# Top-k masks of an attention kernel: another form of the instruction, and all of them on GpSimd

## What is computed

```
q, k = layernorm(q), layernorm(k)              # over the 8 columns of a head
scores = q @ k.T / sqrt(8)                     # 256 x 256 for each batch and head
aw = softmax(scores)
kth = top_k(aw, 12)[..., -1:]                  # int(256 * 0.05) = 12
aws = aw * (aw >= kth)                         # keep the 12 largest of each row
o_s = (aws / (aws.sum(-1) + 1e-8)) @ v
```

## Time and profile before

| | us |
|---|---|
| median of 3 runs | 1230.13 (1228.34 to 1232.35) |
| the profiled execution, whole | 1228.88 |
| its span, first instruction to last | 1226.5 |
| busy: VectorE | 1187.3 (97%) |
| busy: ScalarE | 1086.7 (89%) |
| busy: GpSimd | 1083.7 (88%) |
| busy: TensorE | 962.0 (78%) |
| DMA, mean share of its 16 engines | 22.9% |

### The profile page before, as it was taken

How to read it: one execution, slowest core, us unless ns; L and a number is a source line. 1 busy time by engine, 2 the same in 40 slices (tenths; PEclk the granted TensorE clock), 3 DMA queues, 4 the chain that set the end, 5 groups by cost and what they waited for, 6 DMA issues and landing times.

```text
span 1226.5 us, 34671 instructions
## 1 busy us (share of the span) xinstructions
PE 962.0 (78%) x8997; PEld 653.9 (53%) x9028; DVE 1187.3 (97%) x4553; ACT 1086.7 (89%) x3626; POOL 1083.7 (88%) x1688
## 2 busy tenths in 40 slices
PE   2577878877788788788787878778887888788786
PEld 1255555555556555565555555555555555555554
DVE  6699999999999999999999999999999999999994
ACT  2498999999999999999999989999999999999984
POOL 4599999999999999999999999999999999999964
PEclk9999999999999999989999999999999999999989
DMA  2122212222221222221222221222222122222110
GB/s 62 48 74 79 83 46 65 61 80 83 83 70 43 67 70 83 83 79 41 71 60 83 83 84 45 66 58 83 83 83 65 50 66 71 83 83 79 38 52 14
DMA packets 165143, 82.78 MB, mean 67 GB/s; under 512 B 7753, under 2 KB 164943, under 8 KB 164946
## 3 DMA queue, kind: packets, MB, share of 16 engines
q1 hardware_dynamic: 164946, 80.56, 22.9%
HBM read 42.78 MB, written 37.75 MB: 66 GB/s over the span
## 4 chain that ended last, share of the span: by engine, by line
DVE 60%; issue 26%; PE 4%; DVEq 4%; POOL 3%; ACT 2%; SPq 0%; DMA 0%; POOLq 0%; ACTq 0%
DVE rest L539 26%; DVE top L532 20%; DVE next L545 8%; DVEq L75 4%; POOL below L386 2%; PE turn_ps L834 1%; DVE o_sparse L587 1%; ACT e L717 1%; DVE lin_z L560 1%; DVE den L584 1%; PE pv_ps L855 0%; PE turn_ps L835 0%; DVE stats L595 0%; PE work_ps L932 0%; DVE den L579 0%
## 5 line engine op out<-in xcount | busy, mean ns | idle before, releaser
L386 POOL TENSOR_SCALAR below<-e,next 128x256 bf16<-128x256 f32 x800 | 725.8, 925 | 0.5 <-issue 0.4
L717 ACT ACTIVATE e<-score_ps,drop 128x256 f32<-128x256 f32 x1024 | 472.9, 481 | 57.1 <-POOL drop L364 53.8
L834 PE MATMUL turn_ps<-ident,e 128*128 128x128 f32 x2048 | 401.0, 289 | 40.6 <-ACT kept L687 17.8
L539 DVE MATCH_REPLACE8 rest<-e 128x256 f32<-128x256 f32 x1024 | 409.7, 402 | 0.0
L545 DVE MAX8 next<-rest 128x8 f32<-128x256 f32 x1024 | 403.1, 406 | 0.6 <-issue 0.3
L835 PE MATMUL turn_ps<-minus_huge,below 128*128 128x128 bf16 x2048 | 380.1, 225 | 0.0
L532 DVE MAX8 top<-score_ps 128x8 f32<-128x256 f32 x1024 | 358.4, 408 | 6.8 <-PE score_ps L816 6.6
L834 PEld LDWEIGHTS turn_ps<-ident,e 128*128 128x128 f32 x2048 | 297.6, 145 | 78.9 <-issue 33.0
L687 ACT ACTIVATE kept<-turn_ps 128x1024 f32<-128x1024 f32 x256 | 267.8, 1046 | 39.3 <-PE turn_ps L835 38.9
L835 PEld LDWEIGHTS turn_ps<-minus_huge,below 128*128 128x128 bf16 x2048 | 222.3, 109 | 0.8 <-issue 0.2
L717 ACT ACTIVATION_READ_ACCUMULATOR e<-score_ps,drop 128x1 f32 x1024 | 217.4, 212 | 0.0
(11 more groups left out here) (156 smaller groups left out, 1333.2 us busy)
## 6 DMA issues: line engine op xcount, KB each, us to landing
part_slots<-part SPq DMA_DIRECT2D x128, 192.0 KB, 2.3
q_slots<-part_slots SPq DMA_DIRECT2D x64, 256.0 KB, 3.3
k_slots<-part_slots SPq DMA_DIRECT2D x64, 256.0 KB, 4.1
part_slots<-part SPq DMA_DIRECT2D x64, 128.0 KB, 1.9
x_sb<-in_L_attn_x SPq DMA_DIRECT2D x32, 128.0 KB, 4.2
x_res<-in_L_attn_x SPq DMA_DIRECT2D x32, 128.0 KB, 4.1
out_y<-out_sb SPq DMA_DIRECT2D x32, 128.0 KB, 4.4
w_ops<-in_L_ffn_W SPq DMA_DIRECT2D x1, 512.0 KB
```

Of the source, the lines that this page charges most:

```text
L386: nc.gpsimd.tensor_scalar(below[:, r, t, :], e[:, r, t, :], next8[:, r, t, TOPK - 9:TOPK - 8], None, ALU.is_lt).then_inc(s["below_pool"], 1)
L539: nc.vector.match_replace(rest[:, t, :], e8[:, (u_ - 1) % 2, t, :], e[:, (u_ - 1) % RING, t, :], REMOVED).then_inc(s["rest_ready"], 1)
L717: nc.scalar.activation(e[:, u_ % RING, t, :], score_ps[:, u_ % 2, t // 2, t % 2, :], ACT.Exp, bias=drop[:, u_ % 2, t, 0:1], accum_out=z[:, ...
L834: mm(dst, e[:, r, t, keys], ident[:], start=True, stop=False, is_transpose=True)
```

## The change

All masks go to GpSimd, and ScalarE's are removed. The form for nearly all units, called `gap`: for each tile `gap` = e x (-1) + limit (one instruction with two operations, bf16 result), a wait until the four are done, then one instruction for the unit: `below` = max(gap, 0) over 4 x 256 columns. So `below` is zero or positive, as ScalarE's form was. The first four units of the run use four other forms:

- unit 0, `least`: min(e, limit) - limit, one instruction a tile; the result is zero or negative, so `turn` multiplies with a diagonal of +2^40, the new constant `plus_huge`;
- unit 1, `compare`: (e < limit) x 1.0, one instruction a tile;
- unit 2, `clamp`: `gap` as above, then min(max(gap, 0), 2^40) over the unit;
- unit 3, `wide`: `gap` by one subtraction of two tensors over the unit, the limit repeated along the columns, then max(gap, 0).

`gap` has two buffers. TensorE waits for one count, `below_ready`, instead of two.

```diff
-POOL_TILES = (3, 2, 3, 4, 4, 4, 3, 2)
+FIRST_FORMS = ("least", "compare", "clamp", "wide", "gap", "gap", "gap", "gap")
...
+            nc.gpsimd.memset(plus_huge[:], 0.0).then_inc(s["pool_step"], 1)
+            select(plus_huge[:], ALU.not_equal, HUGE, 0, [[-1, P]], 1, 9).then_inc(s["gather_ready"], 1)
...
-                        for t in range(POOL_TILES[r]):
-                            wait_alone(pool, s["next_ready"], TILES * (g - 2) + t + 1, s["waits_passed"])
-                            nc.gpsimd.tensor_scalar(below[:, r, t, :], e[:, r, t, :],
-                                                    next8[:, r, t, TOPK - 9:TOPK - 8], None,
-                                                    ALU.is_lt).then_inc(s["below_pool"], 1)
+                        form = FIRST_FORMS[r] if g - 2 < UNITS else "gap"
+                        if form in ("least", "compare"):
+                            for t in range(TILES):
+                                limit = next8[:, r, t, TOPK - 9:TOPK - 8]
+                                pool.wait_ge(s["next_ready"], TILES * (g - 2) + t + 1)
+                                if form == "least":
+                                    nc.gpsimd.tensor_scalar(below[:, r, t, :], e[:, r, t, :], limit, limit, ALU.min,
+                                                            ALU.subtract).then_inc(s["below_ready"], 1)
+                                else:
+                                    nc.gpsimd.tensor_scalar(below[:, r, t, :], e[:, r, t, :], limit, 1.0, ALU.is_lt,
+                                                            ALU.mult).then_inc(s["below_ready"], 1)
+                        else:
+                            half = u_ % 2
+                            if form == "wide":
+                                pool.wait_ge(s["next_ready"], TILES * (g - 1))
+                                nc.gpsimd.tensor_tensor(gap[:, half], next8[:, r, :, TOPK - 9:TOPK - 8].to_broadcast(
+                                    [P, TILES, N]), e[:, r], ALU.subtract).then_inc(s["gap_step"], 1)
+                            else:
+                                for t in range(TILES):
+                                    pool.wait_ge(s["next_ready"], TILES * (g - 2) + t + 1)
+                                    nc.gpsimd.tensor_scalar(gap[:, half, t, :], e[:, r, t, :], -1.0,
+                                                            next8[:, r, t, TOPK - 9:TOPK - 8], ALU.mult,
+                                                            ALU.add).then_inc(s["gap_step"], 1)
+                            gaps = 4 if g - 2 == 2 else 5 if g - 2 == 3 else TILES * (g - 1) - 11
+                            pool.wait_ge(s["gap_step"], gaps)
+                            if form == "clamp":
+                                nc.gpsimd.tensor_scalar(below[:, r], gap[:, half], 0.0, HUGE, ALU.max,
+                                                        ALU.min).then_inc(s["below_ready"], TILES)
+                            else:
+                                nc.gpsimd.tensor_scalar(below[:, r], gap[:, half], 0.0, None,
+                                                        ALU.max).then_inc(s["below_ready"], TILES)
...
-                        act.wait_ge(s["next_ready"], TILES * (g - 1))
-                        for t in range(POOL_TILES[r], TILES):
-                            nc.scalar.activation(below[:, r, t, :], e[:, r, t, :], ACT.Relu, scale=-1.0,
-                                                 bias=next8[:, r, t, TOPK - 9:TOPK - 8]).then_inc(s["below_act"], 1)
...
-                    pe.wait_ge(s["below_pool"], POOL_SUM * batch + POOL_UPTO[r + 1])
-                    wait(pe, s["below_act"], (UNITS * TILES - POOL_SUM) * batch + TILES * (r + 1) - POOL_UPTO[r + 1])
+                    far = plus_huge if g2 < UNITS and FIRST_FORMS[r] == "least" else minus_huge
+                    pe.wait_ge(s["below_ready"], TILES * (g2 + 1))
...
-                                last = mm(dst, below[:, r, t, keys], minus_huge[:], start=False, stop=True)
+                                last = mm(dst, below[:, r, t, keys], far[:], start=False, stop=True)
```

More of the change, by code:

```diff
@@ L57 @@
 ROWS = len(SLOTS) * D
-POOL_TILES = (3, 2, 3, 4, 4, 4, 3, 2)
-POOL_SUM = sum(POOL_TILES)
-POOL_UPTO = tuple(sum(POOL_TILES[:v]) for v in range(UNITS + 1))
+FIRST_FORMS = ("least", "compare", "clamp", "wide", "gap", "gap", "gap", "gap")
 RING = 8
@@ L113, in build @@
         minus_huge = sb("minus_huge", [P, P], BF16)
+        plus_huge = sb("plus_huge", [P, P], BF16)
         minus_one = sb("minus_one", [P, P], BF16)
@@ L188, in build @@
         e = sb("e", [P, RING, TILES, N])
+        gap = sb("gap", [P, 2, TILES, N], BF16)
         below = sb("below", [P, RING, TILES, N], BF16)
@@ L206, in build @@
             scores_ready top_ready rest_ready next_ready drop_ready e8_ready waits_passed
-            exp_done below_pool below_act turn_ready turn_copied pv_ready pv_copied
+            exp_done gap_step below_ready turn_ready turn_copied pv_ready pv_copied
             x_stats x_mean x_rsqrt_step x_rsqrt_ready x_newton xn_ready
@@ L722, in body @@
                         nc.scalar.activation(e8[:, u_ % 2], drop[:, u_ % 2, :, 1:9], ACT.Exp).then_inc(s["e8_ready"], 1)
-                    if exists(it if u_ >= 2 else it - 1):
-                        r = (u_ - 2) % RING
-                        act.wait_ge(s["next_ready"], TILES * (g - 1))
-                        for t in range(POOL_TILES[r], TILES):
-                            nc.scalar.activation(below[:, r, t, :], e[:, r, t, :], ACT.Relu, scale=-1.0,
-                                                 bias=next8[:, r, t, TOPK - 9:TOPK - 8]).then_inc(s["below_act"], 1)
                     if u_ % 2 == 0 and exists(it if u_ >= 6 else it - 1):
@@ L823, in turn @@
                     r = (u_ - 4) % RING
-                    batch = it if u_ >= 4 else it - 1
-                    pe.wait_ge(s["below_pool"], POOL_SUM * batch + POOL_UPTO[r + 1])
-                    wait(pe, s["below_act"], (UNITS * TILES - POOL_SUM) * batch + TILES * (r + 1) - POOL_UPTO[r + 1])
+                    far = plus_huge if g2 < UNITS and FIRST_FORMS[r] == "least" else minus_huge
+                    pe.wait_ge(s["below_ready"], TILES * (g2 + 1))
                     wait(pe, s["turn_copied"], g2)
@@ L928, in early @@
                             pe.wait_ge(s["pool_const"], 7)
-                            pe.wait_ge(s["gather_ready"], 4)
+                            pe.wait_ge(s["gather_ready"], 5)
                         for t in range(NT):
```

## The result

| | before | after |
|---|---|---|
| median | 1230.32 us (1228.34 to 1232.35) | **1663.03 us** (1662.72 to 1664.48) |
| ratio | | **1.352** (95% interval 1.351 to 1.354) |
| the profiled execution | 1228.88, span 1226.5 | 1662.72, span 1661.0 |

The change makes the kernel 433 us slower. The forecast was 1229.3 us; rival 1, a new instruction at the pace of `is_lt`, had 1700.

A forecast was written before the change was run, and what follows sets the result against it. VectorE was taken as the bound. GpSimd's unit of 1.54 + 0.20 + 1.03 = 2.77 us stayed under 3.03, so only the tail's -0.8 us counted: 1229.3 us, own range 1226 to 1234, 1226 to 1710 with rivals.

The forecast's parts named there:

- rival 1: GpSimd's maximum or multiply-and-add runs at `is_lt`'s pace, 4.86 to 4.89 us a unit: about 1700 us, chance 0.27.
- What bounds the kernel before: VectorE sets the pace throughout, 36.38 us a batch of 8 units; the change touches none of its instructions.
- GpSimd's allowance of 3.03 us a unit: GpSimd's mask time a unit before it becomes the bound; each further microsecond a unit costs 256 us of run.
- ScalarE's relief: Removing ScalarE's 224 masks, 108.0 us busy in the run, some 3.4 us a batch, was costed at no gain.
- set-up free: Making `plus_huge` takes 204 + 292 ns before GpSimd's first work on `x_rsqrt`, where it waits 0.75 us: nothing.
- the tail step: At the run's end, four old masks of 3.6 us become one new unit of 2.8: 0.8 us gained.
- The cover for uneven units: In the heaviest stretch `drop` comes 1.0 us late; 2.3 us of slack before VectorE needs the exponentials hides it.
- The first four units: The other forms cost at most 3.7 us a unit; 0 to 1 us once, taken as 0.
- The multiply-and-add: GpSimd's instruction on 256 columns takes 401 ns at 0.823 ns a column; four in a row 1.54 us.
- the limit from memory: Reading the multiply-and-add's limit from memory adds 4 ns over a constant; the far bound was `is_lt`'s 926 ns.
- Rival 2: Reading the limit adds 0.07 to 0.15 us a tile, or the maximum is 1.5 to 2 times costlier: 1234 to 1440, chance 0.24.
- The maximum: GpSimd's maximum over 1024 columns takes 1.03 us at the multiply-and-add's pace, 3.15 at `is_lt`'s; 1.03 taken, weakly held.

The follow-up runs named there:

- no_max: The changed kernel with `gap` form for all units, the multiply-and-add writing the mask itself, maximum and its wait left out: 1226.91 us, ratio 0.9985.
- max_one_tile: The changed kernel with `gap` form for all units, the maximum taken of only one tile in four: 1226.89 us, ratio 0.9976.
- no_row_max: The kernel before without VectorE's row maximum `d_max` and GpSimd's subtraction `d_sub` ahead of the small softmaxes: 1205.03 us, ratio 0.981.
- the probe: The kernel before with 13 GpSimd instructions run four times after its last batch, to price each form: multiply-and-add 0.41 us, multiply alone 0.85 on 256 columns.
- relieved: byte_mask with VectorE's input statistics moved to ScalarE and GpSimd, and its reciprocal of `k_sum` to ScalarE: 1228.84 us, ratio 0.999.
- byte_mask: no_row_max with all masks on GpSimd by multiply-and-add, written as an unsigned byte into the bf16 mask's high byte, no maximum: 1205.67 us, ratio 0.981.
- all_is_lt: The changed kernel with all four tiles of every unit masked in the old form, one `is_lt` against the limit each: 1368.08 us, ratio 1.113.

## Why the prediction was wrong, step by step

- **What bounds the kernel before: right.** `no_max` and `max_one_tile` stay at VectorE's time, and taking VectorE's work away in `no_row_max` gains.
- **GpSimd's allowance of 3.03 us a unit, and 256 us of run beyond it: right.** The runs give 3.04 to 3.06 and 252.
- **ScalarE's relief worth nothing, set-up free: right within 3 us**, by `max_one_tile` at 2.64 us a unit. Its gain (0.24%, 2.9 us) is larger than the 0.8 us of the tail step, and the rest has no cause that was tested. **The cover for uneven units** was hardly tried at that cost and stays open.
- **The first four units: too cheap.** The bound was 3.7 us each; they take 4.5 to 5.7. The pairs with a minimum, a maximum or a comparison in them cost more than `is_lt` alone. It is a few us of the 433.
- **The multiply-and-add: slope right, the limit from memory mis-sized.** The pair with constants takes 0.41 us (401 ns taken), with the limit 0.479. I had 4 ns for reading it, from a product of two tensors on two columns; it is 0.07 us, 0.28 a unit. With the maximum as cheap as I took it this alone would have made 1.85 + 0.17 + 1.04 = 3.06 us a unit, at the allowance: the margin of the forecast was gone without the maximum. Rival 2 named this extra (0.07 us a tile); the upper end of its range, 3.85 us a unit, follows from neither of its two cases (3.4 and 3.6).
- **The maximum: this is the step that failed.** I took 1.03 us of the range 1.03 to 3.15; it is 2.77. With it a unit costs 4.75 us in place of 2.8, and by the recorded allowance that is 256 x (4.75 - 3.03) = 440 us, against 433 measured. The reason that I gave for the low end, that a maximum makes no 0-or-1 result and so stands near the arithmetic, sorted instructions by their operation. In the probe this sorting does not hold: a multiplication alone costs the same as the maximum, 0.85 us. The row that said so was in my hand: the one-operation multiply at 227 ns against the pair's 192 on two columns. I wrote that a form with one operation may run by other code, and still took the low end. The 35 ns looked small; behind them stands a slope of 2.50 ns a column ((2770 - 850) / 768 for the maximum), where I had only `is_lt`'s 2.89.
- **The rule of the Trainium skill** (GPSIMD Engine Reference, section 3.1, 1.03 cycles an element for at most two operations) holds in these runs for multiply-and-add, (1040 - 410) / 768 = 0.82 ns a column against the estimate of 0.86. It does not hold for the maximum, 2.50 ns a column, and the other forms of `tensor_scalar` take as long as the maximum or longer on 256 columns.
- **Rival 1: right in mechanism and bound**, 1700 for a measured 1663, and 1635 with a larger fixed part. The measured time lies between them. The chances were not: slower had 0.54 in all, but as the likeliest case I named "same" at 0.42, where the only row of the trace with this size and kind spoke for rival 1.

## What to carry to other kernels

Price an instruction by a row of the same form (how many operations, which pair, operand from memory or constant), not by its kind of arithmetic; where a two-column row of one form is slower than that of another, ask at once what the slope behind it is. A budget drawn from one stretch of the trace (what the second-fullest engine may spend a unit before it becomes the bound) was right to 0.03 us and turned one price into the time; so the price deserved the care. And where one engine is full from end to end, look for work to take from it: one small row maximum gained 25 us, 18 of them as load and 7 because others waited for it at the start, while making room on the two others gained nothing. It does not always work: `relieved` took another 1.1 us a batch from VectorE and was 23 us slower, for a cause that was not found.

## What the runs showed of the hardware

- GpSimd's `tensor_scalar` on 128 x 256: multiply-and-add 0.41 us; multiply, maximum or `is_lt` alone 0.85; multiply-and-maximum, subtract-and-multiply or maximum-and-minimum 1.08. On 1024 columns 1.04 and 2.77. A limit from memory adds 0.07. A subtraction of two tensors takes 0.61 on 256 columns, quicker than a multiplication by a constant alone.
- Its write to an unsigned byte can stand for the maximum: `byte_mask` rests on negatives becoming 0 and large positives 255. With a stride of two bytes the instruction takes 482 ns against 479 in bf16, with about 0.09 us idle before each.
- TensorE's granted clock fell with its work: 0.81 from 400 to 700 us after the change against 0.97 before, a mean over its levels of 1.2 and 2.4 GHz, with 1679 products in the stretch instead of 2316, and a 128 x 128 transpose took 337 ns in the mean instead of 289. It shows no part in the time: in the stretch it is 0.92 in `all_is_lt` and 0.81 after the change, and GpSimd's cost a unit gives both times with one allowance, within 5 us.
